# Graph edges in two streams, summed in pairs on two blocks of weight columns, the second layer's last steps beside the experts

## The reference

```python
# graph branch, twice: h0 = xn, h1, h2
m   = h[src] * rel[edge_type]
m   = concat(m[:half] @ W_in, m[half:] @ W_out)
agg = segment_sum(m / max(deg, 1)[dst], dst)
h   = h + res * tanh(agg + h @ W_loop + b)
# the branch's result: h2 @ mu_w + mu_b
# mixer branch, four layers: linear attention, then a feed-forward of 1024 columns
# x = x + graph + mixer; then on layernorm(x): shared MLP and the best two of four experts
```

## Time and profile before

| | us |
|---|---|
| median of 3 runs | 1943.48 |
| lowest and highest run | 1941.87, 1944.0 |
| span of the profiled execution | 1937.8 |

### The profile page before, as it was taken

One profiled execution on the slowest core, in us unless ns is written; L12 is line 12 of the kernel. 1 busy time (PEld: TensorE's weight loads), 2 busy tenths in 40 slices (PEclk: granted clock), 3 DMA queues, 4 the chain that ended last, 5 costly groups with the idle time before them and its releaser, 6 DMA issues.

```text
span 1937.8 us, 28847 instructions
## 1 busy us (share of the span) xinstructions
PE 1821.0 (94%) x9176; PEld 1505.8 (78%) x9176; DVE 1248.8 (64%) x3345; ACT 632.8 (33%) x1552; POOL 1322.3 (68%) x1301
## 2 busy tenths in 40 slices
PE   2899899999899999999999789998899999999999
PEld 1567787887588888768888667876788888888998
DVE  6786465674855576486466645868765666654766
ACT  4452233343323333332333222332121211223443
POOL 6777777777777777777777757777777777770000
PEclk9999999999999999999999989999999999999999
DMA  9568666667776666687677856667766766661000
GB/s 274 177 198 258 203 191 206 186 202 222 243 209 199 204 194 198 208 249 214 193 218 220 274 190 229 190 200 224 229 182 215 209 199 200 190 181 17 15 28 28
DMA packets 194575, 371.44 MB, mean 192 GB/s; under 512 B 37993, under 2 KB 126095, under 8 KB 194430
## 3 DMA queue, kind: packets, MB, share of 16 engines
q0 software_dynamic: 77632, 223.91, 40.6%
q1 hardware_dynamic: 92228, 126.68, 19.9%
q10 hardware_dynamic: 24570, 19.04, 3.4%
HBM read 305.39 MB, written 64.95 MB: 191 GB/s over the span
## 4 chain that ended last, share of the span: by engine, by line
PE 80%; DVE 8%; issue 3%; DMA 3%; POOL 2%; SPq 2%; ACT 2%; DVEq 0%; ACTq 0%
PE ps_down L2765 16%; PE ps_hid L2753 16%; PE ps_seg L2629 15%; PE ps_kv L2662 5%; PE ps_x L2717 4%; PE ps_x L546 3%; PE ps_hid L3229 2%; PE ps_kv L3082 2%; POOL xg L959 2%; PE ps_hid L2682 1%; DVE xg L1055 1%; PE ps_kv L2795 1%; PE ps_down L2795 1%; DMA h_rows<-qT_all 1%; PE ps_hid L3220 1%
## 5 line engine op out<-in xcount | busy, mean ns | idle before, releaser
L959 POOL DMA_INDIRECT xg<-h_rows,idx_tab x416 | 437.2, 1051 | 143.3 <-issue 114.0
L906 POOL DMA_INDIRECT rg<-relation_rows,idx_tab x416 | 426.7, 1026 | 133.5 <-issue 126.1
L959 POOL DMA_INDIRECT xg<-xn_rows,idx_tab x416 | 423.4, 1018 | 131.9 <-issue 120.3
L2629 PE MATMUL ps_seg<-xg,hot 128*125 128x257 f32 x1664 | 414.8, 382 | 19.7 <-DVE xg L1055 19.5
L2753 PE MATMUL ps_hid<-hT,wff 128*128 128x250 f32 (+1 forms) x1920 | 368.3, 341 | 1.0 <-issue 0.8
L2629 PEld LDWEIGHTS ps_seg<-xg,hot 128*125 128x125 f32 x1664 | 305.3, 188 | 75.0 <-DVE xg L1055 19.2
L2765 PE MATMUL ps_down<-wff,gT 128*125 128x256 f32 x1600 | 363.6, 381 | 0.0
L2753 PEld LDWEIGHTS ps_hid<-hT,wff 128*128 128x128 f32 x1920 | 312.8, 189 | 37.9 <-issue 7.9
L1055 DVE TENSOR_TENSOR xg<-xg,rg 128x512 f32<-128x512 f32 x416 | 285.8, 687 | 70.8 <-DMA rg<-relation_rows,idx_tab 52.0
L2765 PEld LDWEIGHTS ps_down<-wff,gT 128*125 128x125 f32 x1600 | 295.2, 188 | 41.3
L2204 ACT ACTIVATE gT<-ps_hid,b1p 128x250 f32<-128x250 f32 (+1 forms) x480 | 177.8, 433 | 291.6 <-PE ps_hid L2753 291.5
(11 more groups left out here) (378 smaller groups left out, 2385.5 us busy)
## 6 DMA issues: line engine op xcount, KB each, us to landing
second_relation_rows<-rg SPq DMA_DIRECT2D x104, 512.0 KB, 4.1
rg<-second_relation_rows SPq DMA_DIRECT2D x104, 512.0 KB, 4.1
wff<-L_mix_W ACTq DMA_DIRECT2D x8, 1024.0 KB
rg<-relation_rows,idx_tab POOLq DMA_INDIRECT x416, 3.5
xg<-xn_rows,idx_tab POOLq DMA_INDIRECT x416, 3.2
xg<-h_rows,idx_tab POOLq DMA_INDIRECT x416, 3.6
h_rows<-qT_all SPq DMA_DIRECT2D x25, 112.0 KB
qrow<-h_rows ACTq DMA_DIRECT2D x25, 112.0 KB
```

The costliest lines, as they stand in the source:

```text
L906: pool.indirect_dma_start(rg[:, k, :], None, rel_d, bass.IndirectOffsetOnAxis(ap=idx_tab[:, step, 1:2], axis=0))\
L959: pool.indirect_dma_start(xg[:, k, 0:D], None, rows, bass.IndirectOffsetOnAxis(ap=idx_tab[:, step, 0:1], axis=0))\
L2629: ins = pe.matmul(ps_seg[u // UW % 2][0:T, 0:AW], hot[:, s % HOTS, :], xg[:, s % RING, :], start=s % WIN == 0, stop=s % WIN == WIN - 1)
```

## The change

The rows of a node tile are split in two strips of 64 and 61. Strip 0 of tile t holds nodes 64t onward of the first 1600, strip 1 nodes 1600 + 61t onward; rows move between DRAM and a tile in three pieces (0 to 64, 64 to 112, 112 to 125) instead of two. The edges run in two streams, the first half of the list and the second, and a unit is two steps of each. TensorE sums a step of the first stream into rows 0 to 63 of a bank, with 64 weight columns, and a step of the second into rows 64 to 124, with 61. Edges of the second stream whose nodes still lie in strip 0 (its first 12 steps) go through an extra matmul into another bank. A window is six pairs, and its blocks are added to the accumulator by masks worked out ahead, at fixed rows. The first half's weights are W_in, the second's W_out, strip by strip, so a tile's product is two whole-width matmuls (W_loop) and two pairs.

The step tables are new: 24 steps instead of 40 lie among the passage's tiles, one unit every third tile from tile 3, the passage is still behind layer 2's third group, and the second layer's last 104 steps lie in the expert loop, in its first twelve iterations. `dense_beside` starts 18 slots later and ends in the expert loop. The expert weights are loaded early, into the half of `rg` that the second layer no longer uses; that layer's relations have 16 slots instead of 32. x is loaded again by ACT's queue and added by VectorE, not by POOL's accumulating DMAs. The experts use fewer banks (their third layer one instead of two).

```diff
 RING = 16
-HOTS = 8
 SLOTS = 3
-UNIT = 2
-WIN = 8
+CUT = 112
+UNIT = 4
+HOT_UNITS = 2
+ROUND = 2
+WIN = 6
 BLOCK = 4
 HEADSTART = 16
 STORE_AT = (2, 5)
-CUT = 112
+STRIPS = ((0, 64), (64, T))
+WIDTH = tuple(z - a for a, z in STRIPS)
+DRIFT = 24
 AHEAD = 6
 STEPS_FRONT = (0, 8, 8, 8, 8)
-STEPS_JOINT = (14, 14, 14, 36)
-STEPS_GROUP = ((20, 26, 24, 24, 24), (20, 24, 24, 24, 22), (18, 24, 68, 48, 54), (58, 58, 58, 56, 48))
-AMONG, AMONG_AT = 20, 2
+STEPS_JOINT = (16, 16, 16, 32)
+STEPS_GROUP = ((16, 24, 24, 24, 24), (16, 24, 24, 24, 24), (24, 40, 48, 24, 24), (24, 52, 52, 52, 52))
+STEPS_LAST = 104
+AMONG, AMONG_AT, AMONG_EVERY = 6, 3, 3
 DENSE_LAYER, DENSE_GROUP = 2, 3
+LAG = 18
...
+    def blocks_of(w):
+        r, end = windows[w]
+        found = set()
+        for j in range(2):
+            low = nominal(j, r) - DRIFT - BASE[j]
+            high = min(nominal(j, r) + DRIFT + WIDTH[j] - 1, nominal(j, end) + DRIFT) - BASE[j]
+            if high >= 0:
+                found.update(range(max(int(low // WIDTH[j]), 0), min(int(high // WIDTH[j]), NT - 1) + 1))
+        return range(min(found), max(found) + 1)
...
+    add_list, in_tile_at, adds_upto = [], [], []
+    for w in range(WINS):
+        in_tile_at.append(len(add_list) - (1 if w > 1 else 0))
+        add_list += [(w, b) for b in blocks_of(w)]
+        if w == 1:
+            add_list.append((w, REST_ROW))
+        adds_upto.append(len(add_list))
...
+    PIECES = ((0, 64), (64, CUT), (CUT, T))
+    def tile_rows(dram, t, a, z):
+        j = int(a >= STRIPS[1][0])
+        return dram[ds(BASE[j] + WIDTH[j] * t + (a - STRIPS[j][0]), z - a), :]
...
+        LAST_SLOT = 2 * NB + 3
+        SPREAD, EDGES_END = 11, 12
+        def last_slots(s):
+            def upto(s):
+                if s <= SPREAD:
+                    return DENSE_SLOTS + s * (2 * (4 * GT + 1) + 3 - DENSE_SLOTS) // SPREAD
+                return min(upto(SPREAD) + 2 * (s - SPREAD), LAST_SLOT)
+            return range(upto(s - 1), upto(s)) if s <= NT else ()
+        def last_units(s, part):
+            return min(STEPS_LAST // UNIT, -(-STEPS_LAST // UNIT * (2 * s - 1 + part) // (2 * EDGES_END)))
...
         def among(t):
-            return min(max(t - AMONG_AT + 1, 0), AMONG)
+            return min(max((t - AMONG_AT) // AMONG_EVERY + 1, 0), AMONG)
...
-        def move(eng, dst, src, done):
-            for rows in (slice(0, CUT), slice(CUT, T)):
-                eng.dma_start(dst[rows], src[rows]).then_inc(done, 16)
+        def move_tile(eng, rows, dram, t, done, store=False):
+            for a, z in PIECES:
+                ends = rows[a:z], tile_rows(dram, t, a, z)
+                eng.dma_start(*(ends[::-1] if store else ends)).then_inc(done, 16)
...
+            def load_relations(u):
+                sp.wait_ge(s_msg, UNITS + (u + 1) + 1)
+                sp.dma_start(rg2[:, u % RU * BLOCK:(u % RU + 1) * BLOCK, :].rearrange("p s d -> p (s d)"),
+                             rel2_d[u:u + 1].rearrange("o p n -> p (o n)")).then_inc(s_r2ld[u % RU], 16)
...
-            def add_x(gi):
-                pool.wait_ge(s_xr, NG * L + gi + 1)
-                pool.wait_ge(s_emz, (gi + 1) * GT)
-                for rows in (slice(0, CUT), slice(CUT, T)):
-                    pool.dma_start(x_rows(gi)[rows], group_rows(io["x"], gi)[rows], accum_op=ALU.add).then_inc(s_er[gi], 16)
...
                     k, g = self.done, self.g
                     self.done += 1
-                    if k % UW == 0 and k:
-                        self.row_numbers(k // UW - 1)
                     at = k * UNIT
                     s = at % RING
-                    hs = at % HOTS
-                    dve.wait_ge(s_seg, g * UNITS + (k + 1 + RU - HOTS // UNIT))
-                    dve.tensor_tensor(hot[:, hs:hs + UNIT, :], iota_t[:, :].unsqueeze(1).broadcast_to([EP, UNIT, T]),
-                                      key_tab[:, at:at + UNIT].unsqueeze(2).broadcast_to([EP, UNIT, T]), ALU.is_equal)
+                    hs = k % HOT_UNITS * UNIT
+                    dve.wait_ge(s_seg, g * UNITS + (k + 1 + RU - HOT_UNITS))
+                    dve.tensor_tensor(hot[:, hs:hs + UNIT, :], iota_t[:, :].unsqueeze(1).broadcast_to([EP, UNIT, WIDTH[0]]),
+                                      key_tab[:, at:at + UNIT].unsqueeze(2).broadcast_to([EP, UNIT, WIDTH[0]]), ALU.is_equal)
+                    if k * PER < EXTRA:
+                        hs = k % HOT_UNITS * PER
+                        dve.tensor_tensor(hot_extra[:, hs:hs + PER, :],
+                                          iota_t[:, :].unsqueeze(1).broadcast_to([EP, PER, WIDTH[0]]),
+                                          extra_keys[:, k * PER:(k + 1) * PER].unsqueeze(2).broadcast_to([EP, PER, WIDTH[0]]),
+                                          ALU.is_equal)
                     m, r = xg[:, s:s + UNIT, 0:D], rg[:, s:s + UNIT, 0:D]
                     if g == 0:
                         dve.wait_ge(s_edge[k % RU], (k // RU + 1) * (2 * 16 * UNIT))
                     else:
-                        dve.wait_ge(s_edge[k % RU], (k // RU + 1 + 2 * (STEPS2 // RING)) * (16 * UNIT))
-                        dve.wait_ge(s_r2ld[at // BLOCK % len(s_r2ld)], (at // (2 * RING) + 1) * 16)
-                        r = rg2[:, at % (2 * RING):at % (2 * RING) + UNIT, :]
+                        dve.wait_ge(s_edge[k % RU], (k // RU + 1 + 2 * (UNITS // RU)) * (16 * UNIT))
+                        dve.wait_ge(s_r2ld[k % RU], (k // RU + 1) * 16)
+                        r = rg2[:, s:s + UNIT, :]
                     dve.tensor_tensor(m, m, r, ALU.mult).then_inc(s_msg, 1)
-                    if k % UW in (2, 3) and k > UW:
-                        self.add(k // UW - 1, k % UW - 2)
+                    while self.adds < adds_before(k):
+                        self.add()
+                    for _ in range(2):
+                        if self.adds < ADDS and last_unit(add_list[self.adds][0]) <= k - 2:
+                            self.add()
...
+                    if self.lay == L - 1:
+                        dve.wait_ge(s_x5, (self.gi + 1) * MOVED)
+                        dve.tensor_tensor(x5, x5, x_again, ALU.add).then_inc(s_er, 1)
+                        dve.wait_ge(s_er, self.gi + 1)
...
                     u = self.done
                     self.done += 1
-                    if u % UW == 0:
-                        pe.wait_ge(s_acc, (self.g * WINS + u // UW) * 2 + 1)
+                    w = window_of(u)
+                    r, end = windows[w]
+                    if u * PER == r:
+                        pe.wait_ge(s_acc, self.g * ADDS + adds_before(u) + 3)
                     pe.wait_ge(s_msg, self.g * UNITS + (u + 2 + RU))
-                    for s in range(u * UNIT, (u + 1) * UNIT):
-                        ins = pe.matmul(ps_seg[u // UW % 2][0:T, 0:AW], hot[:, s % HOTS, :], xg[:, s % RING, :],
-                                        start=s % WIN == 0, stop=s % WIN == WIN - 1)
+                    for i in range(PER):
+                        now = u * PER + i
+                        for j, (a, z) in enumerate(STRIPS):
+                            part = j * PER + i
+                            ins = pe.matmul(ps_seg[bank_of(w)][a:z, 0:AW], hot[:, u % HOT_UNITS * UNIT + part, 0:z - a],
+                                            xg[:, u % RU * UNIT + part, :], start=now == r, stop=now == end - 1)
+                    for i in range(PER):
+                        now = u * PER + i
+                        if now < EXTRA:
+                            ins = pe.matmul(ps_seg[1][0:WIDTH[0], 0:AW], hot_extra[:, u % HOT_UNITS * PER + i, :],
+                                            xg[:, u % RU * UNIT + PER + i, :], start=now == 0, stop=now == EXTRA - 1)
                     ins.then_inc(s_seg, 1)
...
+            def tile_product(bank_rows, sums, g):
+                for c in range(KC):
+                    pe.matmul(bank_rows(0, T), sums(KC + c), wg[g][2][:, c, :], start=c == 0, stop=False)
+                for c in range(KC):
+                    for j, (a, z) in enumerate(STRIPS):
+                        ins = pe.matmul(bank_rows(a, z), sums(c)[:, a:z], wg[g][j][:, c, :], start=False, stop=c == KC - 1)
+                return ins
...
             dve.wait_ge(s_ew, 16 * LAST_LOADS)
+            upto, _ = edges.stage(at_last, 1)
             for s in range(1, NT + 2):
+                slots = last_slots(s)
                 gi, j = last_part(s)
+                if gi and j == 0:
+                    logits(gi)
+                    shift_logits(gi)
+                upto(last_units(s, 0))
+                for slot in slots[:len(slots) // 2]:
+                    dense_beside(slot)
                 if s <= NT:
                     gated_rows(s - 1)
                 if s == 1:
                     last(dve.tensor_tensor(eb3_all, eb3_all, b2_b[:, :].unsqueeze(1).broadcast_to([T, NX, D]), ALU.add))
+                upto(last_units(s, 1))
```

(4 more changed lines are left out.)

722 lines of the change are left out of this document (383 added, 339 removed).

## The result

The kernel after takes **2038.77 us** (median of 4 runs, 2036.79 to 2041.16), the kernel before 1942.67 on the same chip (4 runs, 1940.04 to 1944.0): ratio 1.0511, 95% interval 1.0485 to 1.0536. It is 96 us slower, where 33 less were forecast, with a range up to 1970. The profiled execution after has a span of 2035.4 us (before 1937.8).

What follows compares the result with a forecast made beforehand. It took POOL's gathers to set the time up to 1133 us and TensorE behind 1150; -5 (first half) + 10 (passage) - 58 (edges) + 9 (node tiles) + 10 (last stage) = -34 from 1943.5 gave 1910 us, range 1855 to 1970.

Steps and rivals of the forecast that it cites:

- Edges behind the passage, -58: Second-layer edge matmuls on TensorE: paired halves overlap, 106 + 12 + 5 us replace 181; -58, ends -86 and +29.
- Rival B: Edge matmuls: the halves of a pair run one behind the other, over 1.6 us a unit; total 2001 us, chance 0.18.
- Rival E: Edge matmuls: weight loads of one half hold up the other's matmuls, 44 us more; total 1954 us, chance 0.04.
- Node tile product, +9: 25 node tiles behind the passage: one slot more each on TensorE plus two changes of width; +9 us (5 to 14).
- First half, -5: Up to the passage: POOL's 832 gathers stay the same, only some waits go; -5 us (0 to -12).
- VectorE, 0: VectorE's one-hot compares take 85 us less, but all lies beside TensorE or POOL; 0 us.
- Passage, +10: Between layers: six tiles instead of three follow the last unit, partly offset by other work first; +10 us (0 to +20).
- Last stage, +10 (0 to 60): Expert loop's first 12 iterations: TensorE, VectorE and POOL, nearly equally loaded, wait on each other; +10 us (0 to +60).
- D: Expert loop stalls: TensorE waits behind VectorE for the same unit, 60 us instead of 10; total 1960 us, chance 0.10.
- The sum itself: Whole kernel: the terms -5 + 10 - 58 + 9 + 10 make -34 us, giving 1910 us; chance 0.52.
- C, POOL sets the end: Behind the passage: overlap is fuller and POOL's gathers set the end; total 1870 us, chance 0.16.
- the forecast's own signs: Unit about 1.1 us; last first-layer gather within 12 us of 1132; second-layer gathers first near 1165, last near 1760.

Runs made afterwards that it cites:

- twice-issued run: Changed kernel with each second-layer unit's edge matmuls issued twice over; 2072.63 us, ratio 1.0671 to the kernel before.
- the best run: Changed kernel with one-pair units taken two at a time, 40 steps among the passage, earlier norms, SP's DMA issues strewn, 104 steps beside the experts; 1946.24 us, ratio 1.0035.

## Why the prediction was wrong, point by point

*Edges behind the passage, -58.* **Right in sum, by luck in its parts.** The halves of a pair run wholly beside each other, so a run of n units takes 4n slots and not 4n+1: 16 us of the forecast's 106 were not there. The changes of width cost more than I took: 0.15 us inside a lone unit and 0.19 to 0.2 on its whole-width neighbours, together the upper end, for which I had named the drain of the Trainium skill's "TensorEngine Tiling (Array Packing)", Key Properties; the trace agrees with that price (0.34 a run for 0.326). The trace has 90 such runs where I counted 74, so the changes cost some 31 us for 12. 90 for slots, 31 for changes and 5 for the extra matmuls are 126, for 123 forecast; all TensorE's work behind the passage fell by 47 us at full clock. Rival B falls: a lone unit takes 1.02 us, not 1.74. Rival E falls too: starts stay 0.217 apart, with loads of 64 columns beneath them.

*Node tile product, +9.* Right: some 51 us for 44.5 at full clock, +6.

*First half, -5, and VectorE, 0.* **Wrong**, +22. The step that failed is the one that put VectorE at nothing because it "lies beside TensorE or POOL". It lies beside POOL, which sets this half, and gathers under VectorE's two-input instructions are longer: with multiplies of twice the length their excess grows by 21 us (56 to 77), 12 of it under the multiply itself. The first gather is also 3 us later (24.81 for 21.57). The run with units of one pair takes the 21 back.

*Passage, +10.* **Wrong**, +31 on top of that. I counted the tail from TensorE's last unit, at tile 18, and matched 24 steps with 18 tiles at 3.6 us. But POOL runs up to a full ring ahead: with four units of lead, one in three tiles, its last gather started when some 11 tiles were done (37 us behind the first product at 1118, at 3.4 a tile). The 14 others and the stores follow at 3.3 to 3.4 us a tile, of which SP's queue holds 3.1 for the moves and a relation store of 0.58 every third tile. And SP's price for a third piece was scaled from two (2.3 us for load and store) where 3.06 was to come. The run with ten units gives 23 of it back in the tail.

*Last stage, +10 (0 to 60).* Mis-sized, +43. That it stalls on VectorE, as D has it, was right; I gave it its low end, and D named the wrong place. Idle time from layer 3's last group on is 40 us for 10, and half clock costs 16 us for 3. Of TensorE's waits there only 6 us are on a unit's multiply, 20 on the normalised rows of a group. The run with earlier norms ties 16 to this place, which I had not seen: the rows of a group's norm are made one iteration ahead of their turn, where they were made two.

*The sum itself* failed at a step that I took over from the kernel before without writing it down: that behind the passage TensorE would go on to set the time when its work got less. It set it before, with 25 us idle; 47 us less work is more than that margin. The twice-issued run shows that in layer 3's groups most of what the pairs save is worth nothing. Ahead of the last stage, idle time (33 us more) and half clock (16 more) had no term at all, and these 49 us, with the three misses above (27, 21 and 33 beyond their terms), make up the 132 between forecast and result. What is late there is, by the waits, the lockstep of the ring: POOL waits for TensorE to free a unit's slots, VectorE for POOL's gathers, TensorE for VectorE. That units of four make each wait longer is argued from runs that change more than the unit; no run isolates it. Units of one pair, with corrections, bring TensorE's idle time from 88 to 59 us. Half clock behind the passage costs 32 us in all, 3 in the kernel before.

*C, POOL sets the end*: false as put. POOL never ran without waits (31 us against a full ring in the run nearest to it); the runs with 26 and with no steps beside the experts are slower.

Of the forecast's own signs, the unit's length came true, the last first-layer gather (1154.56), the first second-layer gather (1208.26) and the last one (1902) did not, and the passage was later than 1175.

Not settled: which of VectorE's orders makes the other 34 us of idle time in the best run, and what pairs give by themselves, since no run has this layout with halves that exclude each other.
